# Attention and routing batches: next tokens requested inside q's stacking, statistics and root steps at other places, two of six low parts computed by VectorE

## What is computed

```python
xn = _layernorm(x)
x  = x + attention(xn) + experts(xn)

# attention: 16 heads of 16, 128 random features per head
q_p = elu(einsum('bhnd,hdf->bhnf', q, proj)) + 1.0
k_p = elu(einsum('bhnd,hdf->bhnf', k, proj)) + 1.0
kv   = einsum('bhnf,bhnd->bhfd', k_p, v)
attn = einsum('bhnf,bhfd->bhnd', q_p, kv) * 1/(einsum('bhnf,bhf->bhn', q_p, k_p.sum(2)) + 1e-8)
out  = attn @ W_out.T + b_out

# experts: top 2 of 8, exact gelu
weights = softmax(where(logits >= second_largest, logits, -inf))
out = einsum('etd,te->td', gelu(xf @ W1 + b1) @ W2 + b2, weights)
```

## Time and profile before

| | |
|---|---|
| median of the runs | 700.1 us (699.58 to 700.13) |
| time of the profiled execution | 700.86 us |
| its span, first to last instruction | 698.7 us |
| outside the span | 2.16 us |
| mean granted TensorE clock | 0.996 of full speed |
| TensorE matmul busy | 682.9 us, 98% |
| VectorE busy | 504.1 us, 72% |
| ScalarE busy | 475.3 us, 68% |
| one batch of the loop, unit 0 to unit 0 | 35.02 us |

### The profile page before, as it was taken

The page is one execution under the profiler, slowest core; times in us unless marked ns, Lnnn a source line. Parts: engine busy times, 40 slices in busy tenths (PEclk is TensorE's granted clock), DMA queues, the critical chain, the costliest instruction groups (busy, mean ns, idle before and its releaser), DMA issues.

```text
span 698.7 us, 17362 instructions
## 1 busy us (share of the span) xinstructions
PE 682.9 (98%) x5503; PEld 603.3 (86%) x5504; DVE 504.1 (72%) x1246; ACT 475.3 (68%) x875; POOL 227.9 (33%) x169
## 2 busy tenths in 40 slices
PE   8899999999999998999999999999999999999996
PEld 4666777777777776589999999999999999999996
DVE  8798888888888878748577675556777545577544
ACT  5687969696969696776557775447775444577553
POOL 2053232323232324643232532225233222322422
PEclk9999999999999999999999999999999999999999
DMA  8856474747474647765455663336556333454531
GB/s 266 200 182 170 108 228 106 228 106 228 106 228 106 198 106 223 224 189 142 100 98 118 145 167 46 46 47 106 178 71 167 48 52 53 81 131 107 69 48 23
DMA packets 87205, 91.65 MB, mean 131 GB/s; under 512 B 60049, under 2 KB 73361, under 8 KB 84897
## 3 DMA queue, kind: packets, MB, share of 16 engines
q1 hardware_dynamic: 71426, 59.36, 33.9%
q0 software_dynamic: 13872, 18.75, 15.2%
q10 hardware_dynamic: 1872, 13.11, 5.1%
HBM read 39.32 MB, written 26.67 MB: 94 GB/s over the span
## 4 chain that ended last, share of the span: by engine, by line
PE 82%; DVE 6%; issue 4%; ACT 2%; POOL 2%; DMA 2%; SPq 1%; POOLq 0%; DVEq 0%
PE F L527 9%; PE F L528 9%; PE F L529 9%; PE WK L527 5%; PE F L596 5%; PE WK L529 4%; PE WK L528 4%; PE NUM L527 4%; PE NUM L529 4%; PE NUM L528 4%; PE DEN L605 4%; PE DEN L527 4%; PE DEN L529 4%; PE DEN L528 4%; PE F L590 3%
## 5 line engine op out<-in xcount | busy, mean ns | idle before, releaser
L1932 POOL DMA_INDIRECT out<-ysb,icur x75 | 121.0, 1613 | 270.6 <-DVE ysb L1763 241.0
L1218 ACT ACTIVATE h<-F,b1c 128x384 f32<-128x384 f32 x200 | 112.2, 575 | 140.0 <-PE F L529 131.2
L1740 DVE TENSOR_TENSOR hl<-h,hh 128x768 fp32r<-128x768 f32 x100 | 96.1, 962 | 111.6 <-ACT hh L1222 111.6
L1063 ACT ACTIVATE e_ring<-F 128x512 f32<-128x512 f32 x256 | 145.7, 621 | 38.5 <-PE F L590 35.0
L527 PE MATMUL F<-gxh,wh 128*128 128x384 f32 (+1 forms) x400 | 128.6, 321 | 0.4 <-DVE wl L1641 0.4
L528 PE MATMUL F<-gxl,wh 128*128 128x384 f32 (+1 forms) x400 | 128.0, 320 | 0.0
L529 PE MATMUL F<-gxh,wl 128*128 128x384 f32 (+1 forms) x400 | 128.0, 320 | 0.0
L1866 POOL DMA_INDIRECT xg<-rows,slots x64 | 63.2, 988 | 174.0 <-PE F L590 158.8
L1468 DVE SCALAR_TENSOR_TENSOR kp<-F,e_ring 128x512 f32<-128x512 f32 x128 | 82.7, 680 | 13.2 <-PE DEN L605 6.2
L1468 DVE SCALAR_TENSOR_TENSOR qp<-F,e_ring 128x512 f32<-128x512 f32 x128 | 85.2, 683 | 8.5 <-ACT e_ring L1063 7.0
L1222 ACT ACTIVATE hh<-h 128x768 fp32r<-128x768 f32 x100 | 84.6, 846 | 3.3
(11 more groups left out here) (261 smaller groups left out, 1552.6 us busy)
## 6 DMA issues: line engine op xcount, KB each, us to landing
wraw<-experts ACTq DMA_DIRECT2D x12, 1024.0 KB, 6.2
gblk<-xg SPq DMA_DIRECT2D x100, 96.0 KB
Sk<-kdh SPq DMA_DIRECT2D x64, 128.0 KB, 2.3
Sq<-qdh SPq DMA_DIRECT2D x64, 128.0 KB
xin<-x SPq DMA_DIRECT2D x8, 512.0 KB, 5.5
Sk<-kdl SPq DMA_DIRECT2D x32, 128.0 KB, 2.4
Sq<-qdl SPq DMA_DIRECT2D x32, 128.0 KB
xres<-x SPq DMA_DIRECT2D x8, 512.0 KB
```

Source lines behind the costliest of these rows:

```text
L1063: A(e_ring[:, u % 4, :], F[u % 4][:, :], ACT.Exp, bias=EXP_BIAS, scale=1.0 / DOWN).then_inc(exp_done, 1)
L1218: A(h32[:, m, :], F[m % 4][:, 0:T], ACT.Gelu, bias=b1c[:, w, m:m + 1]).then_inc(gelu, 1)
L1740: V.tensor_tensor(hl[:, 2 * q:2 * q + 2, :], h32[:, 2 * q:2 * q + 2, :], f32(hh[:, 2 * q:2 * q + 2, :]), ALU.subtract).then_inc(hl_rdy, 1)
L1932: pool.indirect_dma_start(out, bass.IndirectOffsetOnAxis(icur[:, s, :], 0), ysb[:, s, :], None, bounds_check=last_token, compute_op=ALU.ad ...
```

## The change

Five edits, all in the first stage:

1. SyncE: the load of the next tokens stands inside `stack_q`, between its eight DMAs of the high parts and its four of the low parts. `store_o` and `load_xres` stand behind `stack_k` instead of behind `stack_q`, one batch number later in the loop.
2. VectorE: in batches b = 1 to 5 the statistics stand in front of features 8 (two) and 13 (two, with a `join()`), and `norm_var` in front of feature 14. Batch 0 keeps them at 16 to 18.
3. VectorE: the nine root steps stand in front of 19, 20, 27, 28, 29 (two), 30 (two) and 31.
4. Two low parts of six, the first of k (`kdl`) and the first of the heads (`atl`), are VectorE subtractions in front of features 12 and 22. The matmuls `qk_rest(b+1, 0)` and `heads_rest(b-1, 0)` and ScalarE's copies go. The last iteration and the start-up keep theirs.
5. GpSimd: `copy_rows(b + 1)` in front of `add_bias(b - 1)`.

```diff
-    STEPS_AT = {19: (0, 1), 21: (2,), 23: (3, 4), 24: (5,), 25: (6,), 26: (7,), 29: (8,)}
+    STEPS_AT = {19: (0,), 20: (1,), 27: (2,), 28: (3,), 29: (4, 5), 30: (6, 7), 31: (8,)}
...
             stack(sp, Sq, qdh, (0, 2), sq_ld)
+            if tokens is not None:
+                load_x(tokens)
             sp.wait_ge(qkl_rdy, 4 * b + 4)
             stack(sp, Sq, qdl, (1,), sq_ld)
...
-        stack_q(1)
-        with sp.Fori(1, NB - 2) as b:
-            load_x(b + 2)
+        stack_q(1, tokens=3)
+        stack_k(2)
+        stack_q(2, tokens=4)
+        with sp.Fori(2, NB - 3) as b:
             stack_k(b + 1)
+            store_o(b - 2)
+            load_xres(b - 1)
+            stack_q(b + 1, tokens=b + 3)
+        for b in (NB - 3, NB - 2):
+            stack_k(b + 1)
+            store_o(b - 2)
+            load_xres(b - 1)
             stack_q(b + 1)
-            store_o(b - 1)
-            load_xres(b)
-        stack_k(NB - 1)
-        stack_q(NB - 1)
...
                     kv(b, 1)
-                    qk_rest(b + 1, 0)
...
-                    if not first:
-                        heads_rest(b - 1, 0)
                     v_logits(b + 1, 1)
...
-                if u == 11:
-                    qk_lo(b + 1, 0)
...
-                    if not first:
-                        at_lo(b - 1, 0)
...
+        def qk_low(b, i):
+
+            dve.wait_ge(qkh_rdy, 4 * b + i + 1)
+            high, low = ((kdh, kdl), (qdh, qdl))[i // 2]
+            V.tensor_tensor(low[:, i % 2, :], QK_BANK[i][:, :], f32(high[:, i % 2, :]), ALU.subtract).then_inc(qkl_rdy, 1)
+
+        def heads_low(b):
+
+            dve.wait_ge(ath_rdy, 2 * b + 1)
+            V.tensor_tensor(atl[:, 0, :], AT_BANK[0][:, :], f32(ath[:, 0, :]), ALU.subtract).then_inc(atl_rdy, 1)
...
+                if u == 12:
+                    qk_low(b + 1, 0)
+                if u == 22 and not first:
+                    heads_low(b - 1)
                 if ahead:
-                    if u == 16:
+                    if u == (16 if first else 8):
                         norm_stats(b + 2, 0, 2)
-                    if u == 17:
+                    if u == (17 if first else 13):
                         norm_stats(b + 2, 2, 4)
                         join()
-                    if u == 18:
+                    if u == (18 if first else 14):
                         norm_var(b + 2)
...
             send(b)
+            copy_rows(b + 1)
             add_bias(b - 1)
-            copy_rows(b + 1)
```

More of the change, by code:

```diff
@@ L416, in stack_k, with stack_q @@
             stack(sp, Sk, kdl, (1,), sk_ld)
-        def stack_q(b):
+        def stack_q(b, tokens=None):
             sp.wait_ge(qkh_rdy, 4 * b + 4)
@@ L1040, in qk_lo @@
         def qk_lo(b, i):
-            act.wait_ge(qkr_full, 4 * b + i + 1)
+            act.wait_ge(qkr_full, i + 1 if isinstance(b, int) and b == 0 else 3 * b + i + 1)
             A((kdl, qdl)[i // 2][:, i % 2, :], QK_BANK[i][:, :], ACT.Copy).then_inc(qkl_rdy, 1)
@@ L1069, in at_lo @@
         def at_lo(b, g):
-            act.wait_ge(atr_full, 2 * b + g + 1)
+            act.wait_ge(atr_full, {NB - 2: NB - 1 + g, NB - 1: NB + 1 + g}[b] if isinstance(b, int) else b + 1)
             A(atl[:, g, :], AT_BANK[g][:, :], ACT.Copy).then_inc(atl_rdy, 1)
```

## The result

The kernel after the change takes 708.6 us (708.28 to 709.09), the kernel before 699.9 beside it: ratio 1.0119, 95% interval 1.0106 to 1.0131, 8.7 us slower. The forecast was slower, 705.4, with a range up to 708.0: the direction holds, the size is too small, and the time lies 0.6 above the range. The profiled execution of after took 708.28 us, its span 706.1, so the two traces differ by 7.4 us.

What follows compares the result with a forecast made beforehand. TensorE, 98% busy, was taken as the bound, with VectorE's feature 13 delaying unit 17: 5 x 0.97 + 0.10 + 0.3 = 5.25 us on the 700.1 median gives 705.4 us, range 702.0 to 708.0 (82%).

Steps and rivals of the forecast that it cites:

- TensorE is the bound, unit 17 is the tight place: TensorE 98% busy; feature 13, with 0.33 us to spare, ends late, so unit 17 loses 0.97 in batches 1 to 5.
- the forecast's 4.35: Two statistics and a join before feature 13: 0.87 us in each of five batches, 5 x 0.87 = 4.35.
- Two statistics before feature 8 free, tokens in time: Two statistics of 0.74 us fit VectorE's 0.84 wait before feature 8; tokens land by 169.7, before 169.97.
- Removed matmuls not seen: On TensorE, 13 matmuls of 0.23 us go, 3.0 in all, but waits replace them; rival that they are seen: 11%.
- Batch 6: Without statistics there, feature 13 ends at 175.54 and unit 17 starts at 175.59, a loss of 0.10 us.
- Today the bias sum lies over VectorE's statistics, and both have their usual length: GpSimd's moved bias sum: today's lengths, 2.41 and 0.74 us, were taken to speak for 705.4, without contention.
- The estimate beside it: GpSimd's bias sum, held off by VectorE, would double to 4.8 us, giving 707.8 us instead of 705.4.
- 5.25: Total predicted loss in us: 5 x 0.97 for batches 1 to 5, 0.10 for batch 6, 0.3 for batch 0.
- The rival of the late tokens: At the residual, VectorE waits for the bias sum: 0.4 us in a batch, 2.4 more, 707.8 us; chance 9%.
- The first batch: 0.3: Batch 0: feature 13 ends 0.60 later, `kv` starts 0.5 later after unit 17; loss taken as 0.3, between 0 and 0.5.
- The root steps behind feature 26: On VectorE, 0.16 us each and less, standing where it waits anyway: 0.58 us before the residual.
- The clock: Rival: each new TensorE wait of 1.2 us halves the clock, losing 1.7 in five batches, 713.9 us; chance 4%.

Runs made afterwards that it cites:

- e12: Changed kernel with store, residual load and bias sum back in the old order, second session: 728.1 us, ratio to the kernel before 1.0092.
- e13: Changed kernel with statistics back at 16 to 18 and store, residual load and bias sum in the old order, second session: 723.8 us, ratio to before 1.0033.
- b0: The kernel before, unchanged, run again for its trace: 699.7 us.
- b1: The kernel before, unchanged, run once more for its trace: 701.3 us.
- e2: Changed kernel with store, residual load and bias sum back in the old order, first session: 726.0 us, ratio to the kernel before 1.0085.
- e2b: Changed kernel with statistics back at 16 to 18 and store, residual load and bias sum in the old order, first session: 722.0 us, ratio to before 1.0027.
- e5: Kernel before with only the two low-part subtractions in front of features 12 and 22, in place of matmuls and copies: 722.6 us, ratio 1.0042.
- e4: Kernel before with one added small VectorE scaling, one SBUF input, under GpSimd's bias sum: 714.4 us.
- e6b: Kernel before with two low parts on VectorE, in front of features 28 and 30, from batch 1 on: 719.3 us, ratio 0.9977.
- e8: Kernel before with three low parts on VectorE, in front of features 25, 28 and 30, from batch 1 on: 699.8 us, ratio 0.9992.
- e7: Changed kernel with the nine root steps back in front of features 19 to 29, bias sum still late: 707.4 us, ratio to the kernel before 1.0096.
- e6: Kernel before with two low parts on VectorE, in front of features 28 and 30, batch 0 too: 699.6 us, ratio 0.9988.

## Why the prediction was right and wrong

- **TensorE is the bound, unit 17 is the tight place: right.** The wait is there, 4.9 us in five batches, released by the `kp` feature, and the middles are within 0.04 of 0.97 in batches 1 to 5. e12 against e13 prices the statistics at 4.3 us, the forecast's 4.35.
- **Two statistics before feature 8 free, tokens in time: right.** The wait there fell from 0.84 to 0.20.
- **Removed matmuls not seen: right.** 3.0 us were on the table, none came back. With 0.23 taken out in front of units 12 and 22, features 13 and 22 are what is waited for.
- **Batch 6: about right.** 0.21 instead of 0.10.
- **"Today the bias sum lies over VectorE's statistics, and both have their usual length": the step that failed.** The rows were true, and the conclusion was not: they show which instructions are free of the hold (statistics, features and products, of which none has two SBUF inputs), and the edits put other ones there, the root steps and the routing's instructions. The section priced the new place of the bias sum by its own length and the residual's wait, found both harmless, as they were, and never listed what VectorE runs meanwhile. It cost 1.95 us. The estimate beside it had the hold the wrong way round: GpSimd's sum kept its 2.39 us, and VectorE stood. With it the sum is 5.25 + 1.95 = 7.2, against 7.4 in the two traces. On the median that would have been 707.3 us, inside the range; the last 1.3 us are the difference between the profiled executions and the medians, of which the next item shows a part. The rival of the late tokens (0.4 in each of six batches, 2.4 us) comes near the 1.95 by luck: it had the residual wait for the bias sum, and the residual waited for nothing.
- **The first batch: 0.3 was too small, and the two traces hide it.** In both the granted clock is 0.50 for 3.4 us of batch 0. In two further traces of the kernel before (b0, b1) it isn't, though b0's TensorE was busy for the same 1.46 us of the 3.00 ahead. The row of b0 for the stretch in which the first trace has 0.50:

```profile
27.00:30.40 3.40, 3.11 (x26) 2.62 (x24) 3.26 (x17) 2.61 (x7) 0.00 (x0) 1.00 0.78 177
```

Units 5 to 17 of batch 0 take 10.79 and 10.80 us there, and 11.52 in the first trace. Without such a stretch the kernels with the subtraction in front of feature 12 take 11.33 (e2, e2b, e5), those without it 10.79 to 10.81 (b0, b1, e4, e6b, e8): 0.53 more, the forecast's 0.5 for unit 17, which it then took as 0.3. Unit 0 of batch 0 comes at 20.58 in the first trace, at 20.16 and 21.00 in b0 and b1, at 20.87 in after. So what after loses up to unit 0 of batch 1 depends on the trace of before beside it: 0.4 us with the first, 1.6 with b0, 0.7 with b1.
- **The root steps behind feature 26, which "stand where VectorE waits anyway": right alone, wrong together.** e12 shows them all but free without the hold, e7 a hold of up to 1.55 us free without them.
- **The clock: right.** Five waits of 1 us left it at 1.00; behind one of 1.87 in e6 it fell. The rival's price was too high: it reckoned 1.7 us for a stretch of 3.40 at half clock, and such a stretch in batch 0 costs 0.73 (11.52 against 10.79).

## What to carry to other kernels

Before a GpSimd instruction is moved, or a load that it waits for, list what VectorE runs in its new place, and look for two SBUF inputs and for one-input scalings from SBUF to SBUF: each such instruction, however small, may last until GpSimd is done. A row in which the two lay over one another unharmed speaks only for the instructions in it. Work taken from a bound engine pays only where the engine that gets it has slack: the same subtraction of 0.60 us lost time in front of the tight features 12 and 22, and in front of 28 and 30 each brought 0.22 us a batch. Two delays that each fit into an engine's slack have to be added before either is called free.

## What was not expected of the hardware

- A 128x4 VectorE instruction of 0.15 us lasted up to 1.99 us beside a GpSimd sum and 2.78 us beside a sum and a copy, with one SBUF input as with two; a reduction of the same tile stayed at 0.147. What TensorE lost was the length of the hold less 1.47 us, in four batches of four.
- A wait of 1.87 us with TensorE busy for 4.69 of the 6.00 us around its start was followed by 3 us at a granted clock of 0.50 and 4 more at 0.53, the 1.2 GHz level; TensorE then was busy without a gap, at half speed. Waits of 0.97, one in a batch, did nothing of the kind.
- The stretch of 3.4 us at half clock in batch 0 comes in some executions and not in others of one and the same kernel, with TensorE busy for the same 1.46 of 3.00 us ahead.
- One program took 719.3 us in one session and 698.5 in another, with 1.7 us of added waits in a batch of the loop and 9.2 in batch 0, whose releaser the trace doesn't show.
